# Reordering three node stages and packing the walk's table reads in a graph network kernel

## What is computed

```python
def layernorm(x):                        # without gain and bias
    return (x - mean(x)) / sqrt(var(x) + 1e-5)

# L0: GraphSAGE: mean of the neighbours' rows
neigh = segment_sum(x[src], dst) / maximum(degree, 1)
x = layernorm(x + concat([x, neigh]) @ W_neigh + b_neigh)

# L1: two GCN2 layers, folded: segment sums of scaled rows over src and back, then one matrix
h = segment_sum(norm * x[col], row); xp = 0.9 * h + 0.1 * x
x = (1 - beta) * xp + beta * (xp @ W)    # twice; then layernorm(x_in + x)

# L2: GATv2 over the edges, then per node
x1 = layernorm(x + h) * g1 + beta1
f = gelu(x1 @ W1.T + b1) @ W2.T + b2
x = layernorm(x_in + layernorm(x1 + f) * g2 + beta2)

# L3: two GAT layers; only h3 = x @ W and its attention terms are made in the third node stage
```

## Time and profile before

| | us |
|---|---|
| median of 3 executions | 7529.38 (7518.4 to 7531.32) |
| profiled execution | 7521.0, span 7519.1 |
| walks e0, e1a, e1b | about 454 to 1075, 1546 to 2170, 2171 to 2790 |
| node stage n0 (blocks in steady state) | 1120 to 1520 |
| node stage n1 (the same) | 2820 to 3100 |
| node stage n2 (the same) | 4530 to 5350 |
| busy over the span | PE 3962.8, DVE 3333.9, ACT 2255.2, POOL 3670.1 |

### The profile page before, as it was taken

How to read it: one execution, slowest core, us unless ns; L and a number is a source line. 1 busy time by engine, 2 the same in 40 slices (tenths; PEclk the granted TensorE clock), 3 DMA queues, 4 the chain that set the end, 5 groups by cost and what they waited for, 6 DMA issues and landing times. The chain is left out here.

```text
span 7519.1 us, 103124 instructions
## 1 busy us (share of the span) xinstructions
PE 3962.8 (53%) x21453; PEld 2742.6 (36%) x21454; DVE 3333.9 (44%) x13934; ACT 2255.2 (30%) x6392; POOL 3670.1 (49%) x4923
## 2 busy tenths in 40 slices
PE   4421667733641667456666858888502069602068
PEld 3311656622641655323332226656301057501023
DVE  4310235511210238534456647776505268605368
ACT  0000336511420446422222226666300034300035
POOL 3655015564036004344442547776672745572778
PEclk7555889965875889878888879999755589855589
DMA  1011225523432447541110013333322179622179
GB/s 22 1 46 54 71 93 180 177 79 84 141 106 60 140 141 252 173 157 33 34 30 12 28 48 118 114 119 115 92 59 66 39 239 291 201 61 67 40 251 312
DMA packets 551030, 816.76 MB, mean 109 GB/s; under 512 B 118566, under 2 KB 267629, under 8 KB 550466
## 3 DMA queue, kind: packets, MB, share of 16 engines
q1 hardware_dynamic: 354484, 506.90, 22.3%
q10 hardware_dynamic: 127152, 184.90, 6.6%
q0 software_dynamic: 69184, 122.90, 6.5%
HBM read 493.48 MB, written 329.46 MB: 109 GB/s over the span
## 5 line engine op out<-in xcount | busy, mean ns | idle before, releaser
L619 POOL DMA_INDIRECT agg_dst<-e_rows,e_put_i x392 | 404.5, 1032 | 392.0 <-DVEq L646 273.2
L931 PE MATMUL e1a_bank<-y_rows,e1a_hot 128*128 x1584 | 277.4, 334 | 345.2 <-issue 251.8
L1861 POOL DMA_INDIRECT e_rows<-h,e_other_i x392 | 383.8, 979 | 150.2 <-issue 118.9
L931 PE MATMUL e_bank<-x_rows,e_hot 128*128 x1584 | 274.7, 332 | 344.8 <-issue 239.5
L931 PE MATMUL e1b_bank<-y_rows,e1b_hot 128*128 x1584 | 273.5, 331 | 346.4 <-issue 257.7
L892 POOL DMA_INDIRECT y_rows<-m,s_other_i x196 | 187.7, 958 | 437.9 <-POOLq L101 377.7
L1701 PE MATMUL lg_z_ps<-gat_wl,lg_tr 128*128 128x512 f32 x392 | 246.8, 715 | 275.9 <-DVE lg_at L1757 127.8
L931 PEld LDWEIGHTS e1a_bank<-y_rows,e1a_hot 128*128 128x128 f32 x1584 | 253.0, 235 | 369.9 <-issue 369.4
L931 PEld LDWEIGHTS e_bank<-x_rows,e_hot 128*128 128x128 f32 x1584 | 251.1, 232 | 368.6 <-issue 368.2
L931 PEld LDWEIGHTS e1b_bank<-y_rows,e1b_hot 128*128 128x128 f32 x1584 | 249.7, 232 | 370.3 <-issue 369.7
L1472 POOL TENSOR_TENSOR n_rstd<-n_mv,minus_half 128x4 f32<-128x4 f32 x98 | 104.7, 1069 | 538.3 <-DVE n_mv L1565 538.3
(11 more groups left out here) (511 smaller groups left out, 12267.7 us busy)
## 6 DMA issues: line engine op xcount, KB each, us to landing
n_ag<-agg_dst SPq DMA_DIRECT2D x294, 264.0 KB, 3.9
n_xs<-x SPq DMA_DIRECT2D x294, 256.0 KB, 3.5
h<-n_ho ACTq DMA_DIRECT2D x196, 264.0 KB, 3.4
n_hs<-h SPq DMA_DIRECT2D x196, 264.0 KB
agg_dst<-e_ev SPq DMA_DIRECT2D x196, 132.0 KB
y<-n_o ACTq DMA_DIRECT2D x98, 264.0 KB, 3.7
e1a_fed<-y SPq DMA_DIRECT2D x196, 132.0 KB
m<-e1a_ev SPq DMA_DIRECT2D x196, 132.0 KB
```

Of the source, the lines that this page charges most:

```text
L619: pool.indirect_dma_start(out=agg, out_offset=bass.IndirectOffsetOnAxis(ap=e.put_i[:, c:c + 1], axis=0), in_=rows[:, c, :], in_offset=None ...
L931: ins = pe.matmul(bank[:, bass.ds(to * 512 + h * width, summed)], hot[:, s, k, h * P:(h + 1) * P], rows[:, bass.ds(chunk, 1), 0:summed], s ...
L1861: pool.indirect_dma_start(out=rows[:, c, :], out_offset=None, in_=h, in_offset=bass.IndirectOffsetOnAxis(ap=e.other_i[:, c:c + 1], axis=0))\
```

## The change

It has two parts. In the walks TensorE's load reads the same table as 32-bit values, four a batch, and takes each of the eight 16-bit fields apart with shifts and masks; the two counts for the waits are masked to eight bits. In the node stages only the lags and the orders in `pipeline` change, on all four engines in n0, on three in n1 and on TensorE and ScalarE in n2.

```diff
-                flat = e.table[:, :, :].rearrange("o b w -> o (b w)")
+                flat = e.table[:, :, :].rearrange("o b w -> o (b w)").bitcast(I32)
...
-                            flat[0:1, bass.ds(turn * (HOTS * WORDS) + s * WORDS, WORDS)], engines=[mybir.EngineType.PE],
-                            min_val=0, max_val=RING << 8, skip_runtime_bounds_check_because=why)
+                            flat[0:1, bass.ds(turn * (HOTS * WORDS // 2) + s * (WORDS // 2), WORDS // 2)], engines=[mybir.EngineType.PE],
+                            min_val=0, max_val=RING << 24, skip_runtime_bounds_check_because=why)
                         pe.wait_ge(hot_ready, turn * HOTS + s + 1)
-                        pe.wait_ge(ready, word[STEPB])
-                        pe.wait_ge(begun, word[STEPB + 1])
+                        pe.wait_ge(ready, word[STEPB // 2] & 255)
+                        pe.wait_ge(begun, (word[STEPB // 2] >> 16) & 255)
                         for k in range(STEPB):
-                            chunk = nc.s_assert_within(word[k] & 255, 0, J - 1, skip_runtime_bounds_check_because=why)
-                            to = nc.s_assert_within(word[k] >> 8, 0, RING - 1, skip_runtime_bounds_check_because=why)
+                            two = word[k // 2]
+                            number, place = ((two >> 16) & 255, two >> 24) if k % 2 else (two & 255, (two >> 8) & 255)
+                            chunk = nc.s_assert_within(number, 0, J - 1, skip_runtime_bounds_check_because=why)
+                            to = nc.s_assert_within(place, 0, RING - 1, skip_runtime_bounds_check_because=why)
...
 node_sage
-                pipeline(pool, (0, degree), (3, deviation), (3, factor))
+                pipeline(pool, (0, degree), (4, deviation), (4, factor))
-                pipeline(pe, (2, product), (1, turn_over))
+                pipeline(pe, (2, turn_over), (3, product))
-                pipeline(act, (4, apply), (1, move), (4, store))
+                pipeline(act, (2, move), (5, apply), (5, store))
-                pipeline(dve, (0, mean), (3, sums))
+                pipeline(dve, (1, mean), (4, sums))
 node_gcn
-                pipeline(pe, (2, product), (1, turn_over))
+                pipeline(pe, (1, turn_over), (2, product))
-                pipeline(act, (5, store), (4, apply), (1, move))
+                pipeline(act, (5, store), (1, move), (4, apply))
-                pipeline(dve, (3, sums), (0, mix))
+                pipeline(dve, (0, mix), (3, sums))
 node_gatv2
-                pipeline(pe, (2, ffn1), (6, turn3), (3, ffn2), (7, product3), (1, turn1))
+                pipeline(pe, (2, turn1), (6, turn3), (3, ffn2), (7, product3), (2, ffn1))
-                pipeline(act, (8, store_h), (2, gelu), (5, third_norm), (5, store_x3), (1, first_norm), (6, move3), (7, keep_h),
-                         (1, move1))
+                pipeline(act, (8, store_h), (3, gelu), (2, move1), (5, third_norm), (5, store_x3), (6, move3), (1, first_norm),
+                         (7, keep_h))
```

## The result

The changed kernel takes 7128.1 us (median of 4 runs, 7127.4 to 7145.7) against 7527.7 us for the kernel before (4 runs on the same chip, 7518.4 to 7531.3). The ratio is 0.9477, interval 0.946 to 0.9494: 400 us less, where 321 us less was forecast. The profiled execution has a span of 7125.5 us (before 7519.1).

The account below looks back on a forecast made before the run. Bound by orders of waits, no engine busy throughout a touched stage; TensorE's sequencer paces the walks. Walks -107, node stages -96, -33 and -85 us make -321: 7529.4 to 7208 us; range 7121 to 7400 us.

Parts of the forecast that it names:

- Load: In the walks: four 32-bit values take 0.55 us a load, against 2.23 us for eight of 16 bits.
- rival A: In the walks: the load costs by the count of values, 0.88 to 1.1 us; total 7264 to 7304 us; chance 0.22.
- B: In the walks: the load costs by its width, 16 bytes as before; total 7485 us; chance 0.10.
- D: Slower than before: load by width, nine register instructions at 0.15 us each in the walks; total 7585 us; chance 0.04.
- E: Node stages' copies still come last, orders without effect, the walks alone gain; total 7422 us; chance 0.05.
- Masks: In the walks: nine more register instructions a batch at 0.1 us each, 0.9 us.
- The half clock in the walks: In the walks: a batch takes 5.1 us with the half-clock parts, 5.0 us at full clock.
- During the gathers: In each walk while GpSimd issues gathers: 37 sequencer instructions a batch for 28, so 4.6 batches done in place of 6.
- First node stage: ScalarE, with its store exposed behind the apply, sets the pace at 3.45 us a block; 96 us saved.
- Second node stage: TensorE's wait for the copy goes; 2.80 us a block for 3.15, 33 us saved.
- Third node stage: A chain through two steps, longer than ScalarE's own work, gives 8.2 us a block; 85 us saved.
- C: In the node stages: orders only pass the wait on, 3.9, 3.05 and 8.9 us; total 7339 us; chance 0.16.

Follow-up runs that it names:

- second kernel: Old walks with the new node orders, against the kernel before: 7316.5 us (0.9725).
- e1a_bank, e1a_hot: Not a run: a buffer named in the profile rows of TensorE's weight loads in the walks; no time of its own.
- sixth kernel: Changed kernel with sixteen 32-bit values a load at multiples of 16 bytes, and stores moved behind other work in all three node stages: 6822.6 us (0.9062).
- fourth kernel: Changed kernel with fourteen 32-bit values a load, no decoding, and ScalarE's old orders in the node stages: 7727 us.
- fifth kernel: Changed kernel with eight 16-bit values a load and the extra masks, VectorE's old orders in the first two node stages and GpSimd's in the first: 7541 us.
- eighth kernel: The sixth kernel with VectorE's old order in the second node stage: 6801.0 us (0.9033).
- seventh kernel: Changed kernel with eight 32-bit values at a stride of 40 bytes, and six dummy products on TensorE before the gelu wait in the third node stage: 7166 us.
- ninth kernel: Changed kernel with only the stores of h moved behind gelu and copy; in the second node stage TensorE's old order with six banks: 7063 us.

## Why the prediction was right, and where not

The time fell inside the range, 80 us below the forecast and only 7 us above the range's lower end (7121 us). That it stayed inside is in part luck, since two errors of opposite sign met: the walks gave 206 us where 107 were forecast and 125 was the bound, and the third node stage gave 40 for 85. The first two node stages gave 107 and 34 for 96 and 33. By its steps:

**Load.** Right in kind, 0.33 us for the 0.55 chosen; the bound "Below 0.485 it can't go" was wrong. The prediction had "an aligned row of whole words may come in one go" as a choice; the runs bear out just that: 0.33, 0.6 and 1.1 us at the least for four, eight and sixteen words at multiples of 16 bytes, 2.3 us for the same eight at other places and 2.2 us for eight 16-bit values, so, as an estimate, about 0.27 us for each access of one value or of four whole words. That is how these sizes fit together, not something a trace shows directly. The one 32-bit value of 0.485 us, on which 0.55 was built, is the row that doesn't fit. The Trainium skill's rule (Runtime: NRT & Kernel Launch, Instruction fetch mechanics, 200 ns a register even in bulk), which would have made rival A the likelier, doesn't hold for such words: four registers came in 0.33 us, and the measurement decides. For 16-bit values it is near (2.2 us for eight). Rivals A, B and D fall with the load, and E with the second kernel, whose node orders alone give 210 us.

**Masks.** Count right, price too high: 0.07 us for 0.1 each, 0.6 us a batch for 0.9.

**The half clock in the walks.** The sum carried 0.1 us a batch for it, taken from before's 0.86. It went to 0.98 when the pause of 2.2 us at each load went. The other kernels agree: after the gathers those with a load of 2 us or more in every batch or every second one have 0.82 to 0.88, those with short loads alone 0.98 or 0.99. Load, masks and clock together make 4.64 to 4.72 us a batch in the three walks for 5.1, some 77 us.

**During the gathers.** Wrong. A batch with 37 sequencer instructions in place of 28 should have been slower there, so that 4.6 batches get done in place of 6. Here are TensorE's weight loads and register instructions in the first 269 us, of before, of after, and of the kernel with late stores, whose steps take no value apart:

```profile
L931 PEld LDWEIGHTS e1a_bank<-y_rows,e1a_hot x135: 192/288/338, 1554.1 to 1812.2; 128*128 128x128 f32 x135
...
L931 PEldq FUSED_REGOPS  x69: 7/99/709, 1553.9 to 1811.6; - x69
```

```profile
L933 PEld LDWEIGHTS e1a_bank<-y_rows,e1a_hot x134: 285/333/338, 1380.8 to 1639.0; 128*128 128x128 f32 x134
...
L933 PEldq ALU_OP  x86: 5/700/1410, 1380.4 to 1640.4; - x86
```

```profile
L932 PEld LDWEIGHTS e1a_bank<-y_rows,e1a_hot x135: 186/287/338, 1300.2 to 1559.6; 128*128 128x128 f32 x135
```

The number of weight loads is the same, 134 or 135, whatever stands between them. Six batches get done in each of these kernels, and the seventh load of the walk begins 27 to 29 us after GpSimd issued its last gather. The earlier trace rows were read as a price of each register instruction, and that reading falls. Something paces TensorE there that the decoding doesn't change; what it is stays open, and no run looked for it. It was worth 21 us of the error (1.4 batches of 5.1 us in three walks).

**First node stage.** Right, and for the reason given: the exposed store. ScalarE idles 0.62 us between apply and copy, the stage takes 3.38 us (3.45 forecast), and with the store alone moved (the sixth kernel) it falls to 3.17, with TensorE busy throughout (3.24 was the bound given). VectorE and GpSimd don't slow each other more than before: GpSimd is busy 163.77 us in the 240 of the fourth kernel, 2.2 us a block, where it was 2.60. The rule on the port pair (the Trainium skill, SBUF — State Buffer, section SBUF: two separate sides) had given 3.6 us for the stage; at 3.17 what the rule describes isn't what binds. The fifth kernel shows the other half: with VectorE's and GpSimd's orders undone, 4.56 us.

**Second node stage.** 2.80 us as forecast; by luck in part. The wait for the copy is gone, but the sums of single engines are not what binds. The exposed store was a term of ScalarE's 2.7 us, and with the store moved (the sixth kernel) the stage still takes 2.80. TensorE waits for ScalarE's apply to give a bank free (29.7 us in 79 blocks). VectorE's part of the edit is a loss of 0.16 us a block: without it the stage takes 2.64, and this wait is gone (eighth kernel). That the apply comes late because VectorE's statistics stand behind the mix fits both, but no run gave the changed order more banks.

The waits' view of the changed kernel inside the stage (us in total, times, longest):

```profile
PE n_y_ps L1501 <- ACT n_o L1218: 29.7, 79, 1.1
```

**Third node stage.** The mechanism was right: a chain through two steps, over gelu, FFN product, GpSimd and ScalarE. Here is one turn of it in the changed kernel where the clock was full, from a gelu to the third norm of the next step and from a third norm to the next gelu:

```profile
4407.19 1.27 ACT L2228 ACTIVATE n_gt<-n_f_ps,n_b1g 128x512 f32<-128x512 f32 x2 [1.12 <-PE n_f_ps L2180]
...
4409.80 1.65 ACT L1218 ACTIVATE n_x3s<-n_r,n_shift,n_rstd 128x128 f32<-128x128 f32 x4 [0.85 <-POOL n_shift L1209]
...
4417.59 1.26 ACT L1218 ACTIVATE n_x3s<-n_r,n_shift,n_rstd 128x128 f32<-128x128 f32 x3
```

From the gelu at 4407.19 to the norm at 4417.59 it is 10.4 us (10.0 in the prediction), from the norm at 4409.80 to the gelu at 4415.96 below 6.2 us (6.1). In the mean of the seventh kernel, at full clock, they are 10.2 and 6.2 us; half of their sum is its 8.19 us a block, the forecast's 8.2. The stores lie in the second part: where they move, the first stays at 10.2 us and the second falls to 5.0 (ninth kernel) and 4.6 us (sixth), and half of the sum is 7.58 and 7.38. In the changed kernel itself the two are 10.8 and 6.6 us.

Missed was what the chain does to the clock. TensorE, which before waited at most 1.1 us for its copy, now stands still for each gelu, 1.4 us in the mean and up to 2.1, and ScalarE's gelu stands behind the two stores of h. The waits' view of before and of the changed kernel (us in total, times, longest), then the timeline:

```profile
PE n_f_ps L2178 <- ACT n_xt L2220: 95.0, 90, 1.1
```

```profile
PE n_y_ps L2145 <- ACT n_gt L2228: 124.4, 90, 2.1
```

```profile
4414.46 0.40 ACT L2217 ACTIVATE n_ho<-n_h_ps 128x264 f32<-128x264 f32 x1
...
4415.02 0.34 ACTq L2190 DMA_DIRECT2D h<-n_ho  x1
...
4415.52 0.34 ACTq L2191 DMA_DIRECT2D a<-n_ao  x1
...
4415.96 1.27 ACT L2228 ACTIVATE n_gt<-n_f_ps,n_b1g 128x512 f32<-128x512 f32 x2 [1.10 <-issue]
...
4417.28 0.38 PE L2145 MATMUL n_y_ps<-n_bias_parts,ones_b 3*128 3x512 bf16 x1 [1.94 <-ACT n_gt L2228]
```

The granted clock then falls to 0.94, and some steps run at the half clock, with the FFN product on the chain: their four weight loads take 0.97 us where others take 0.53 in the same timeline.

```profile
4400.92 0.97 PEld L2151 LDWEIGHTS n_y_ps<-n_w,n_gt 128*128 128x128 f32 x4
...
4409.79 0.53 PEld L2151 LDWEIGHTS n_y_ps<-n_w,n_gt 128*128 128x128 f32 x4
```

By the seventh kernel that costs 0.51 us a block, and 46 us between the stage's first and last store (833.3 and 787.4 us); missing were 45 (40 for 85). The dummy products tell that the standing still brings the clock down, and not too much work. Where the stores move, TensorE waits at most 0.8 us for the gelu (sixth kernel), and the clock is full without them.

**Rivals.** C (the orders only pass the wait on) was right in place and wrong in size for the first two stages, and near the truth for the third (8.9 us given, 8.70 measured), though for the clock and not for the stores alone, which were in the forecast's 8.2.

## What to carry to other kernels

A DMA issue on a compute engine belongs behind work that needs nothing of it: here moving the stores gave another 140 us (19 in the first stage, 120 in the third, by first and last store) after the change's node orders had given 210. When orders of several engines are shifted, write down for each ring of banks which engine frees it and what stands ahead of the freeing, since a change to one engine alone can close a circle that is worse than the wait it removes (6.23 us a block for 3.15 in the second stage). Put scalars that an engine loads into registers as 32-bit words at multiples of 16 bytes, and prefer more words to more decoding (3.71 us a batch with sixteen words, 4.64 with four and the masks).

## What the runs showed of the hardware

A register load on TensorE takes 0.33 us for four 32-bit values, 0.6 for eight and 1.1 to 1.6 (median 1.3) for sixteen if they begin at a multiple of 16 bytes, 2.0 to 2.7 us for eight of them at 8 past one, and 2.2 us for eight of 16 bits. In a stage in which TensorE is busy 653 of 780 us and waits 1.4 us in the mean of each block in one place its granted clock is 0.94; six dummy products in that wait brought it to 1.00 and made the stage 6% faster. While GpSimd issues gathers, TensorE gets 134 or 135 weight loads done in 269 us, with 18 instructions of its sequencer a batch as with 37.
